# A gated graph-attention and expert layer on one core: both graph layers on all nodes in plain fp32, then one gather

## What is computed

```python
x = x + tanh(g_xattn[0]) * graph(ctx, adj=layernorm(x), W0, ..., b0, W1, ..., b1)
x = x + tanh(g_ffn[0]) * experts(layernorm(x), Wg1, Wg2, Wup, bup, Wdown, bdown)

def gat_layer(h, adj, W, a_self, a_neigh, b):      # 8 heads of 32
    feat = einsum('nf,hfo->hno', h, W)
    e = leaky_relu(attn_self[:, :, None] + attn_neigh[:, None, :]) - 1e10 * (1 - adj)
    return elu(softmax(e) @ feat + b)              # graph(): two such layers
# experts: 8 experts of width 128, the top 2 by tanh(x Wg1^T) Wg2^T, silu between up and down
```

## Time and profile before

| | us |
|---|---|
| median of 3 runs | 98.81 (98.40 to 101.19) |
| profiled execution | 99.17 |
| its span | 97.4 |
| PE busy | 80.6 (83%) |
| DVE busy | 77.2 (79%) |
| ACT busy | 53.2 (55%) |
| POOL busy | 44.4 (46%) |

### The profile page before, as it was taken

How to read it: one execution, slowest core, us unless ns; L and a number is a source line. 1 busy time by engine, 2 the same in 40 slices (tenths; PEclk the granted TensorE clock), 3 DMA queues, 4 the chain that set the end, 5 groups by cost and what they waited for, 6 DMA issues and landing times.

```text
span 97.4 us, 2003 instructions
## 1 busy us (share of the span) xinstructions
PE 80.6 (83%) x635; PEld 76.7 (79%) x635; DVE 77.2 (79%) x210; ACT 53.2 (55%) x129; POOL 44.4 (46%) x100
## 2 busy tenths in 40 slices
PE   5985745968698496969998999999999999999800
PEld 5974734957597495958897899999999999999700
DVE  5599999879899998799999956877636767889520
ACT  5217568479677775135295778764635655443100
POOL 7913685004613798966297000676100788710000
PEclk9999999999999999999999999999999999999999
DMA  2999970000000000000000000011000030003022
GB/s 42 323 328 344 417 276 1 7 0 3 0 0 0 0 0 0 7 0 3 0 3 0 0 7 0 0 58 53 7 0 0 0 106 2 0 7 108 3 66 65
DMA packets 3179, 5.45 MB, mean 56 GB/s; under 512 B 314, under 2 KB 2522, under 8 KB 2908
## 3 DMA queue, kind: packets, MB, share of 16 engines
q1 hardware_dynamic: 3020, 5.00, 14.1%
q10 hardware_dynamic: 144, 0.26, 1.2%
HBM read 4.22 MB, written 1.05 MB: 54 GB/s over the span
## 4 chain that ended last, share of the span: by engine, by line
PE 34%; DVE 23%; POOL 12%; issue 9%; DMA 7%; ACT 5%; SPq 4%; DVEq 1%; POOLq 0%
DMA wup_sb<-in_wup 7%; DVE hid_lo L1025 5%; PE bank L766 5%; PE bank L724 4%; PE bank L768 4%; POOL hit L355 4%; PE bank L767 4%; PE bank L726 4%; PE bank L725 4%; DVE xn L967 3%; DVE xa L1121 2%; PE bank L741 2%; SPq L284 2%; DVE hid L1017 2%; DVE h_lo L1107 2%
## 5 line engine op out<-in xcount | busy, mean ns | idle before, releaser
L724 PE MATMUL bank<-xt_hi,wup_hi 128*128 128x256 f32 x64 | 19.3, 301 | 2.1 <-ACT elu_exp L512 1.6
L520 ACT CAST hid_hi<-hid 128x256 fp32r<-128x256 f32 x32 | 13.0, 406 | 12.7 <-DVE hid L1017 11.2
L766 PE MATMUL bank<-wdown_hi,hid_hi 128*128 128x256 f32 x64 | 18.4, 287 | 0.4 <-ACT hid_hi L520 0.3
L767 PE MATMUL bank<-wdown_lo,hid_hi 128*128 128x256 f32 x64 | 18.0, 281 | 0.0
L726 PE MATMUL bank<-xt_lo,wup_hi 128*128 128x256 f32 x64 | 18.0, 281 | 0.0
L768 PE MATMUL bank<-wdown_hi,hid_lo 128*128 128x256 f32 x64 | 18.0, 281 | 0.0
L725 PE MATMUL bank<-xt_hi,wup_lo 128*128 128x256 f32 x64 | 17.9, 280 | 0.0
L1017 DVE TENSOR_TENSOR hid<-elu_exp,bank 128x256 f32<-128x256 f32 x26 | 10.9, 418 | 7.2 <-PE bank L741 5.6
L512 ACT ACTIVATE elu_exp<-bank,small_sb 128x256 f32<-128x256 f32 x26 | 12.2, 471 | 7.9 <-PE bank L726 7.8
L1025 DVE TENSOR_TENSOR hid_lo<-hid,hid_hi 128x256 fp32r<-128x256 f32 x32 | 15.4, 482 | 0.1
L724 PEld LDWEIGHTS bank<-xt_hi,wup_hi 128*128 128x128 f32 x64 | 12.1, 189 | 2.8 <-ACT elu_exp L512 1.9
(11 more groups left out here) (151 smaller groups left out, 203.7 us busy)
## 6 DMA issues: line engine op xcount, KB each, us to landing
x_sb<-in_x SPq DMA_DIRECT2D x4, 256.0 KB, 3.8
wup_sb<-in_wup SPq DMA_DIRECT2D x1, 1024.0 KB, 7.0
wdown_sb<-in_wdown SPq DMA_DIRECT2D x1, 1024.0 KB, 9.4
out<-out_sb SPq DMA_DIRECT2D x3, 256.0 KB, 2.1
check_sb<-in_check_w SPq DMA_DIRECT2D x1, 320.0 KB
ctx_sb<-in_ctx ACTq DMA_DIRECT2D x1, 256.0 KB, 3.4
w_sb<-in_w SPq DMA_DIRECT2D x1, 256.0 KB, 4.7
out<-out_sb SPq DMA_DIRECT2D x2, 128.0 KB, 3.1
```

The source lines that it names most:

```text
L520: nc.scalar.copy(hid_hi[:, n % HID_SLOTS, :], hid[:, n % 2, :]).then_inc(hid_hi_rdy, 1)
L724: nc.tensor.matmul(dst, wup_hi[:, c, cols], xt_hi[:, b, c, :], start=(c == 0), stop=False)
L766: nc.tensor.matmul(dst, hid_hi[:, n % HID_SLOTS, part], wdown_hi[:, e, :], start=False, stop=False, skip_group_check=True)
L767: nc.tensor.matmul(dst, hid_hi[:, n % HID_SLOTS, part], wdown_lo[:, e, :], start=False, stop=False, skip_group_check=True)
```

## The change

- Layer 0 and layer 1 run on all nodes of a graph from `ctx` as it is; nothing is gathered ahead of them. `twice_part` now multiplies the one-hot map with itself (bf16, 4 matmuls) into `source`, and `gather` applies it once to the result of layer 1, `z`. For graphs 1 to 3 `z` is split (`z_hi` on ACT, `z_lo` on POOL) and gathered with float32r; for graph 0 in plain fp32.
- `feat0` and `feat1` are plain fp32 matmuls on unsplit operands. b0 is a row of `w0` against a row of ones under ctx. All splits of ctx, w0, h1 and w1 go, and b1's takes their place in `feat1`.
- ctx is loaded transposed in two halves, w0 apart from `small`; ctx (first half), w0, b1 and w1 are issued on ACT's queue, the rest on SP's.
- The norm is an ACT activation with scale `rstd` and bias `shift` (`act_norm`), but for the first tile of graph 0, which stays on DVE; `row_power` on POOL gets two more small instructions for it.
- The scores of graph 0 are worked out on DVE (`dve_route`); those of graphs 1 to 3 stay on POOL.
- `gated` reads the gather's PSUM bank, one instruction a row tile.
- POOL makes the onehot tiles of graphs 1 to 3; all `wup_hi` are made on ACT. ACT loads silu's table ahead of the loop.
- The orders of all engines are rewritten; `gather(2)`, `turn(3)`, `twice_part(3)` and `gather(3)` stand in the expert loop. 16 warm-up matmuls in place of 30. The silu outputs have a buffer of their own. In step e = 0 the up product does its four matmuls on `xt_hi` before it waits for `xt_lo`.

```diff
-WARM_MMS = 30
+WARM_MMS = 16
-SCORE_PLACE = (7, 6, 6, 6)
+SCORE_PLACE = (5, 6, 6, 6)
 # POOL, row_power
-            pool.wait_ge(veps_rdy, nb + 1)
+            nc.gpsimd.tensor_scalar(nmean[:, pair(b)], mv[:, pair(b), 0], -1.0, None, ALU.mult).then_inc(veps_rdy, 1)
+            pool.wait_ge(veps_rdy, 2 * nb + 2)
             nc.gpsimd.tensor_tensor(rstd[:, pair(b)], veps[:, pair(b)], powers[:, 0:C], ALU.pow).then_inc(rstd_rdy, 1)
+            pool.wait_ge(rstd_rdy, nb + 1)
+            nc.gpsimd.tensor_tensor(shift[:, pair(b)], nmean[:, pair(b)], rstd[:, pair(b)], ALU.mult).then_inc(shift_rdy, 1)
 # POOL, order
-            for t in range(2 * C, 3 * C):
+            for t in range(C, 4 * C):
 ...
             wup_part(0)
+            row_power(pool, 0, 0)
             wup_part(1)
-            row_power(pool, 0, 0)
+            z_part(1)
             wup_part(2)
+            z_part(2)
             wup_part(3)
             row_power(pool, 0, 1)
-            scores(pool, 0, 0)
+            z_part(3)
+            wdown_part(0)
             row_power(pool, 0, 2)
-            wdown_part(0)
             wdown_part(1)
             wdown_part(2)
+            row_power(pool, 0, 3)
             wdown_part(3)
             scores(pool, 0, 1)
-            row_power(pool, 0, 3)
 # ACT, order up to the expert loop, in which act_norm(b + 1) is at e = 2 and source_copy(3) at i = 4
+            minus0(0)  exp0(0)  minus0(1)  exp0(1)  turned(0)  minus0(2)  exp0(2)  minus1(0)  exp1(0)
+            minus0(3)  exp0(3)  turned(1)  gates  wup_part(0)  source_copy(1)  minus1(1)  act_norm(act, 0, 0, (1,))
+            exp1(1)  wup_part(1)  act_xt(act, 0, 0)  z_part(1)  wup_part(2)  minus1(2)  exp1(2)  source_copy(2)
+            act_gate(act, 0, 0)  z_part(2)  minus1(3)  act_diff(act, 0, 0)  exp1(3)
+            nc.scalar.preload_act_table(ACT.Silu)
+            wup_part(3)  z_part(3)
 # PE, one plain fp32 product of each kind, and the order
+                    mm = nc.tensor.matmul(both(FEAT0[b])[:, c, :], w0_sb[:, c * P:(c + 1) * P], ctx_sb[:, b * N:(b + 1) * N],
+                                          start=True, stop=True)
+                    nc.tensor.matmul(dst, h1[:, b, c, t * P:(t + 1) * P], w1_sb[:, c, :], start=(c == 0), stop=False)
+                            mm = nc.tensor.matmul(dst, source[:, j, rows], elu_exp[:, b, j, :], start=(j == 0), stop=(j == C - 1))
+            feat0(0)  feat0(1)  turn(0)  feat0(2)  feat1(0, 0)  twice_part(0)  feat1(0, 1)  feat0(3)  turn(1)
+            feat1(1, 0)  gather(0)  twice_part(1)  feat1(1, 1)  turn(2)  feat1(2, 0)  twice_part(2)
+            pe_xt(pe, 0, 0)  feat1(2, 1)  feat1(3, 0)  pe_gate(pe, 0, 0)  feat1(3, 1)  gather(1)
+            pe_experts(pe, 0, {1: [lambda: gather(2), lambda: turn(3)], 3: [lambda: twice_part(3)], 5: [lambda: gather(3)]})
 # DVE, order up to the expert loop, and what stands in it
+            rows_top(0)  rows_onehot(0)  bias_lo  elu0(0)  rows_top(1)  elu0(1)  rows_top(2)  elu0(2)  source
+            elu1(0)  rows_top(3)  elu0(3)  gated(0)  stats(0)  dve_norm(dve, 0)  turned(2)  wg1_parts  elu1(1)
+            dve_xt(dve, 0, 0)  elu1(2)  dve_gate_sum(dve, 0, 0)  dve_logits(dve, 0, 0)  gated(1)  stats(1)
+            bdown_hi  dve_route(dve, 0)  elu1(3)
+            dve_experts(dve, 0, {0: [lambda: wdown_part(0)], 1: [lambda: turned(3), lambda: gated(2)],
+                                 2: [lambda: wdown_part(1), lambda: stats(2)], 3: [pick_copy], 4: [bdown_part, lambda: wdown_part(2)],
+                                 6: [lambda: gated(3), lambda: wdown_part(3)], 7: [lambda: stats(3)], 13: [check_peaks],
```

More of the change, by code:

```diff
@@ L244, in build @@
         SCORE_STEPS = 9
+        FIRST_STEPS = 9
         def pair(b):
@@ L338, in scores @@
             r = pair(b)
-            done = [nb * SCORE_STEPS]
+            done = [(run * (B - 1) + b - 1) * SCORE_STEPS]
+            last = done[0] + SCORE_STEPS
             def link(ins, chained=True):
@@ L367, in scores @@
                                     ALU.subtract).then_inc(score_rdy, 1)
-            assert done[0] == (nb + 1) * SCORE_STEPS
+            assert done[0] == last
         @block.gpsimd
@@ L486, in general @@
                     row_power(pool, 1, b)
-                for b in range(B):
+                for b in range(1, B):
                     scores(pool, 1, b)
@@ L495, in act_xt, with act_norm @@
             nc.scalar.copy(xt_hi[:, b, :, :], both(XT)).then_inc(xt_hi_rdy, 1)
+        def act_norm(act, run, b, tiles):
+            act.wait_ge(shift_rdy, run * B + b + 1)
+            for t in tiles:
+                nc.scalar.activation(xn[:, C * b + t, :], xa[:, C * b + t, :], ACT.Identity, bias=shift[:, C * b + t:C * b + t + 1],
+                                     scale=rstd[:, C * b + t:C * b + t + 1]).then_inc(xn2_rdy, 1)
         def act_gate(act, run, b):
@@ L533, in act_experts @@
                     act_hid(act, run, i - PICK_LAG)
+                if e == 2 and b + 1 < B:
+                    act_norm(act, run, b + 1, range(C))
                 if e == 4 and b + 1 < B:
                     act_xt(act, run, b + 1)
+                for step in extra.get(i, ()):
+                    step()
                 if run == 0 and 12 <= i < 12 + NT:
@@ L856, in feat0 @@
[L856 to L871 removed]
+                    pe.wait_ge(w0_ld, 16)
@@ new lines, in gather @@
+            def gather(b):
+                if b == 0:
+                    pe.wait_ge(h1_rdy, 3)
+                if b == 1:
+                    pe.wait_ge(xa_rdy, C)
+                if b == 0:
+                    pe.wait_ge(source0_rdy, 1)
+                    pe.wait_ge(z_rdy, 1)
+                else:
+                    pe.wait_ge(source_rdy, b)
+                    pe.wait_ge(z_lo_rdy, b)
+                for t in range(C):
+                    dst = bank[:, GATHER[b][t], t * D:(t + 1) * D]
+                    rows = slice(t * P, (t + 1) * P)
+                    for j in range(C):
+                        if b == 0:
+                            mm = nc.tensor.matmul(dst, source[:, j, rows], elu_exp[:, b, j, :], start=(j == 0), stop=(j == C - 1))
+                        else:
+                            nc.tensor.matmul(dst, source_r[:, b - 1, j, rows], z_hi[:, b - 1, j, :], start=(j == 0), stop=False)
+                            mm = nc.tensor.matmul(dst, source_r[:, b - 1, j, rows], z_lo[:, b - 1, j, :],
+                                                  start=False, stop=(j == C - 1))
+                    if b == 0 or t == C - 1:
+                        mm.then_inc(gather_mm, 1)
```

447 lines of the change are left out of this document (215 added, 232 removed).

## The result

| | before | after |
|---|---|---|
| median | 98.81 us (98.40 to 101.19; with a fourth run 98.88) | 103.0 us (102.98 to 103.34) |
| profiled execution, its span | 99.17, 97.4 | 103.34, 101.6 |

The ratio is 1.044, 95% interval 1.039 to 1.049. The executions of most kernels here, the one before among them, fall in two groups some 1.5 us apart: the ratios compare the lower ones, the medians are over all of them, and the profiled executions of e1, e2, e3, e7 and e11 are of the upper group, so that their spans are on the long side.

The account below looks back on a forecast made before the run. PE's gapless full stage (249 matmuls, 29.42 us) could only start earlier: 1.3 us from the first silu plus 1.1 from the loop, 2.4, takes the span from 97.4 to 95.0 and the median to 96.4. Range 93.9 to 99.0.

Parts of the forecast that it names:

- `gather(2)` and `turn(3)` fall into PE's wait for the silu and cost nothing: Expert loop before the third up product: both are covered by PE's idle time; without that cover they cost 1.3 us.
- the start to `xt`: Graph 0's path from `w0` landing at about 4.7 us to `xt_hi` at 21.1, 6.7 us early.
- the stops by the port: POOL's subtracts stop small DVE operations, up to 0.9 and 1.3 us; a bit under half taken, first silu at 31.1.
- Plain fp32 products: `feat0`, `feat1` and `gather(0)`: each 256-column product leaves two records and costs 0.43 us, the upper end of the bound.
- this very rival: Clock stays low on graph 0's path: products cost double, 5.9 us more, 102.3; chance 0.12, shared with another late load.
- both stops at full price: Before the first silu: `ldiff` and first scores stopped for 0.9 and 1.3 us, silu at 32.5, no gain.
- the walk: The new order followed with the trace's durations, from `w0` landing to `elu1(3)` ending at 29.7 and the first silu.
- a rival, at 1.7 us and with 0.06: Clock falls once in PE's gap before the third up product: 98.1; chance 0.06, shared with a late rise.
- the cases of the clock: At the start or gap: late or fallen once, within 2%, chance 0.06; low or another late load, slower, 0.12.
- the late load: At the start: `w0` late by 0.6 us, one way to the lead being spent, 97.7; that rival's chance 0.16.
- The loop, 1.1 us: Third up product to the full stage: 18.3 us in place of 19.4, through fewer waits of PE.
- The full stage and the end: From about 50 us: 29.4 us long again, untouched; norm on ACT and larger `check_peaks` costed at nothing.

Follow-up runs that it names:

- e1: The changed kernel with 26 dummy matmuls filling PE's gap before the third up product: 99.48 us, 1.001 of the kernel before.
- e2: The changed kernel with `elu1(3)` on DVE moved ahead of `stats(1)` and the first scores: 97.58 us, 0.972 of the kernel before.
- e3: The changed kernel with 30 warm-up matmuls in place of 16: 101.38 us, 1.009 of the kernel before.
- e7: e5 with graph 0's scores back on POOL, behind `z_part(3)`, and `SCORE_PLACE[0]` at 7: 98.43 us, 0.986 of the kernel before.
- e11: The changed kernel with `exp1(3)` and `wup_part(3)` ahead of `act_diff(0)` and the table load on ACT: 100.06 us, 0.996 of the kernel before.
- e4: The changed kernel with `w0` issued first on SP's queue, not second on ACT's: 99.46 us, 0.999 of the kernel before.
- e5: The changed kernel with the edits of e4 and e2 together: 96.16 us, 0.971 of the kernel before.
- e10: e5 with e11's order on ACT: 96.29 us, 0.973 of the kernel before.
- e12: e10 with the first scores put behind `turned(3)` and `gated(2)` on DVE: 96.12 us, 0.972 of the kernel before.
- e9: The changed kernel with the edits of e4 and e1 together: 98.48 us, 0.991 of the kernel before.
- e8: e5 with all eight norm tiles on DVE: 98.68 us, 0.996 of the kernel before.

## Why the prediction was wrong

Forecast 96.4, measured 103.0, and outside the range (93.9 to 99.0). The step that failed first of all is "`gather(2)` and `turn(3)` fall into PE's wait for the silu and cost nothing": the wait cost 2.7 us through the clock. With it failed two terms on the way there, the start to `xt` (2.4 us) and the stops by the port (1.0 us). By the steps of the prediction:

*Plain fp32 products, 0.43 us: right.* `gather(0)` takes 1.80 for four, two records each, and e3's first four take 0.43 each. The Trainium skill's "FP8 and Floating Point Precision", section "TensorE Precision Notes", has four passes for true fp32; the trace comes near it, 0.43 against 0.118 us of one float32r product is 3.6 times.

*Start to xt: wrong in two terms.* I had `w0` land at 4.7 us, 5.3 at the latest, from the 4.1 us of a load of like size; the first product started at 6.43. The view of the DMA issues of the changed kernel (KB, us from issue to landing) has it, with the load ahead of it on ACT's queue:

```profile
ctx_sb<-in_ctx_t ACTq DMA_DIRECT2D x1, 128.0 KB, 4.1
w_sb<-in_w ACTq DMA_DIRECT2D x1, 128.0 KB, 5.0
```

It was issued at 1.37 us and took 5.0, where `ctx` of the same size took 4.1; the term was 0.9 us too small, and the issue 0.2 late. In the other traces with this order of loads (e1, e2, e3, e11) it took 4.3 to 4.9, so part of this is the one execution; issued first on SP's queue it took 2.0 to 2.5 (e4, e5, e7 to e10, e12). And I took 0.43 for the products just after the warm-up, though I had the row for the start's level and used it to price this very rival. `h1(0)` was ready at 10.5 and not at 7.9, `xt_hi` at 23.5 and not at 21.1: 2.4 us. e4 gives 3.1 back, e3 1.3.

*The shared port: right mechanism, price halved without a reason.* I had written that both stops at full price give 32.5 and none 30.3, and took 31.1 because no row showed a small operation being stopped. They are stopped at full price: 0.94 for 2 columns where it is 0.16 undisturbed, and 1.0 us on `hit` (e11), 1.8 in all where I took 0.8. There is also a slip in the walk: from 25.7 its own terms add to 30.0 for the end of `elu1(3)`, not 29.7. The 2.4 of the start, 1.0 of the port and 0.3 of the slip are the first silu at 34.8 in place of 31.1. My bound held; I chose badly inside it. What the Trainium skill's "SBUF — State Buffer", section "SBUF: two separate sides", states, that the loser waits for the whole instruction, names no size below which it doesn't, and the trace agrees.

*The gap costs nothing: wrong, and the largest single miss.* I had `gather(2)` and `turn(3)` fall into PE's wait for the silu, 2.3 to 3.5 us of idle time, "and cost nothing". The wait was 3.39, as bounded, and it cost 2.7 us more through the clock (e1). I had this as a rival, at 1.7 us and with 0.06; its size came from 18 slow products, where between 35 and 41 us 27 matmuls ran at the lower level. Alone it would have stayed within 2%. What I missed is that the cases of the clock do not exclude the late load and the port: the stops lengthen the gap (2.36 us in e11, 3.39 with them), and the late start, which leaves the gap as it is, goes in these traces with a longer low stretch behind it (over 6 us, some 3 in e4). The Trainium skill's "TensorE: Matmul & The Clock Gate", section "Why this matters for your kernels", warns of such gaps, and this trace, with its 3.39 us, agrees.

*The loop, 1.1 us: half right.* With the clock up (e1) it takes 18.8 us from the third up product (35.02) to the full stage (53.81), before 19.4, forecast 18.3. No wait at either score transpose, as said; but the 0.43 us after the first `hid` stayed in every version but e7 and e12. The count of work was also low: I had 15.1 us of it in the 19.38 of the kernel before, so 4.3 lost, where the trace, with the ends of matmuls modelled, has PE busy for 17.07, so 2.3 lost:

```profile
32.90:52.28 19.38, 17.07 (x132) 15.78 (x132) 18.27 (x48) 10.45 (x29) 14.68 (x29) 1.00 0.01 2
```

*The full stage and the end: right.* 249 matmuls in 29.4 us, and the norm on ACT hurts nothing there.

The sum of the misses: 2.4 (start) + 1.0 (port) + 0.3 (the slip) + 2.7 (clock) + 0.5 (loop), less 0.3 at the end, is 6.6, and the spans differ by 6.6 (95.0 and 101.6). This divides up one trace. The start, the port and the clock have a run behind them (the start's split between landing and level rests on e3 and e4, whose parts overlap). As cures they don't add: by the ratios e1, e3, e4 and e11 each alone take 3.5 to 4.8% of the time before off the 1.044, and e4 and e1 together (e9) 5.3%. How much of each cure is its own term, and how much is the low stretch that it also shortens, the runs don't separate.

## What to carry to other kernels

An idle gap of the matmul engine that a new order opens ahead of dense work is not free cover: price the products behind it at the lower level, and look for one instruction of another chain (here `elu1(3)`) that can go ahead and close it. When a load is on the path of the first work, issue it first (here 2.0 to 2.5 us to landing in place of 4.3 to 5.0), and keep the warm-up long enough to reach it. When a bound leaves 2 us open, and the row nearest to it speaks for the expensive end, don't halve it; and add up losses that share a cause before giving each a small chance.

## What the runs showed of the hardware

The granted clock reads 1.00 from 6.43 to 10.00 us of the changed kernel, where products take 0.89 us that elsewhere take 0.43. In the start the spacing of the products tells the level, not the column. The length of the warm-up alone doesn't fix that level either. Behind 16 warm-up products and 0.78 to 1.46 us of idle time (e11, e2, e1, after) the first four plain products took 3.8 us each time, the lower level. Behind the same 16 without idle time they took from 1.89 (e7, e10) over 2.1 to 2.4 (e4, e9, e12, e5) to 3.15 us (e8), though PE's order up to there is the same in all of them.

The length of a gap alone does not tell whether the clock falls. In the profiled executions it stayed up behind 1.64 us before and behind 1.39 in every version; it fell behind 2.36 us (e11), 2.69 (e7) and 3.38 to 3.39 (e3, e4, after). But behind the same 3.38 us the low stretch was some 3 us long in e4 and over 6 in e3, and in e12 it fell with no gap over 0.79 us in the ten us ahead of it. e12's stage table:

```profile
37.40:38.20 0.80, 0.02 (x1) 0.00 (x0) 0.80 (x3) 0.47 (x1) 0.72 (x2) 1.00 0.00 0
38.20:39.40 1.20, 1.19 (x10) 1.19 (x11) 1.20 (x3) 0.00 (x0) 1.12 (x3) 1.00 0.00 0
39.40:42.50 3.10, 3.10 (x15) 2.93 (x16) 2.87 (x10) 1.10 (x4) 2.85 (x5) 0.52 0.02 5
```

It also differs between executions of one kernel. The ten of e3, all with the same program, have a mean granted clock from 0.952 (102.3 us) to 0.997 (99.04 us), so in one of them the long low stretch was all but absent. And the kernel before, 1.00 throughout in its profile, has a mean under 0.96 in 19 of the 70 executions that ran beside the experiments. A mean of 0.951 over a span of some 98.7 us is an estimated 9.7 us at the lower level, and only 5.2 us of the span lie behind PE's last product: there the clock was low during work. One profile whose clock is up doesn't show that a kernel keeps it. What decides it stays open; no run here was made to separate it.
